# A fused attention, scan and expert kernel: four expert halves moved into the last scans, and the B and C rows stacked

## What is computed

```
x = x + attention(group_norm(x))                       # one head, 64 wide, softmax over 1024 points
t = tokens(x)
# layer 2, a state-space block on layer-normed tokens
z, xBC, dt = split(rms_norm(ln(t)) @ W_in.T)           # 256 | 256 + 32 + 32 | 8
xBC = silu(sum_k xpad[:, k:k+L] * conv_w[:, k] + b)    # causal, 4 taps, over 320 channels
xs, B, C = split(xBC)                                  # 8 heads of 32; B and C of 32 rows each
state = state * dA_t + (dt_t * x_t) outer B_t ; y_t = state . C_t
t = t + ln(t) + out_projection(rms_norm((y + D * xs) * silu(z)))
# layer 3, eight experts, two of them per token
u = ln(t); t = t + u + sum_e gate[e] * (gelu(u @ w1[e] + b1[e]) @ w2[e] + b2[e])
```

## Time and profile before

| | us |
|---|---|
| median of three runs | 1034.85 (1026.72, 1034.85, 1034.92) |
| profiled execution, its own time | 1039.91 |
| its span on the core | 1037.9 |
| PE busy | 889.0 (86%) |
| DVE busy | 742.6 (72%) |
| ACT busy | 522.2 (50%) |
| POOL busy | 250.3 (24%) |
| mean granted PE clock | 0.928 of 2.4 GHz |

### The profile page before, as it was taken

One profiled execution on the slowest core, in us unless ns is written; L12 is line 12 of the kernel. 1 busy time (PEld: TensorE's weight loads), 2 busy tenths in 40 slices (PEclk: granted clock), 3 DMA queues, 4 the chain that ended last, 5 costly groups with the idle time before them and its releaser, 6 DMA issues.

```text
span 1037.9 us, 19619 instructions
## 1 busy us (share of the span) xinstructions
PE 889.0 (86%) x7534; PEld 693.8 (67%) x7534; DVE 742.6 (72%) x1959; ACT 522.2 (50%) x795; POOL 250.3 (24%) x250
## 2 busy tenths in 40 slices
PE   3788998899887789788989797979788999889997
PEld 1555665655574567676768675757667888778887
DVE  2767677767765477686867777766768878787885
ACT  1534544544575464646464656454325654566543
POOL 0034111011100425242524252527511110011100
PEclk9889999999998679898988898989989999999999
DMA  4530000000000330303030303031000000000001
GB/s 138 178 130 22 20 2 21 21 11 12 21 1 15 57 70 3 71 2 71 2 71 1 72 2 71 2 71 63 2 1 1 22 21 22 1 21 22 21 2 42
DMA packets 30892, 36.13 MB, mean 35 GB/s; under 512 B 4560, under 2 KB 24912, under 8 KB 30800
## 3 DMA queue, kind: packets, MB, share of 16 engines
q1 hardware_dynamic: 29648, 30.68, 12.1%
q10 hardware_dynamic: 1152, 4.19, 1.1%
HBM read 21.50 MB, written 4.98 MB: 26 GB/s over the span
## 4 chain that ended last, share of the span: by engine, by line
PE 57%; DVE 27%; ACT 6%; issue 6%; POOL 2%; DMA 1%; SPq 1%; DVEq 0%; ACTq 0%; POOLq 0%
PE ps L1017 7%; PE ps L689 6%; DVE cacc L1665 4%; PE ps L939 4%; PE ps L768 3%; DVE acc L1942 3%; PE ps L770 3%; PE ps L769 3%; PE ps L676 3%; DVE nmax L1522 3%; PE ps L643 2%; PE ps L930 2%; ACT un L1335 2%; PE ps L890 2%; PE ps L648 2%
## 5 line engine op out<-in xcount | busy, mean ns | idle before, releaser
L1942 DVE SCALAR_TENSOR_TENSOR acc<-ps,comb,acc 128x128 f32<-128x128 f32 x512 | 141.1, 343 | 22.2 <-PE ps L1017 21.7
L1017 PEld LDWEIGHTS ps<-w_f,hid 128*128 128x128 f32 x1024 | 131.2, 191 | 16.4 <-ACT hid L1354 8.0
L1017 PE MATMUL ps<-w_f,hid 128*128 128x128 f32 x1024 | 136.7, 276 | 4.6 <-ACT hid L1354 4.5
L1354 ACT ACTIVATE hid<-ps,b_f 128x512 f32<-128x512 f32 x128 | 86.2, 685 | 107.6 <-PE ps L770 107.5
L1522 DVE TENSOR_REDUCE nmax<-ps 128x1 f32<-128x1024 f32 x64 | 78.1, 1221 | 39.7 <-PE ps L648 39.3
L559 POOL TENSOR_TENSOR srs<-sve,neg_half 128x1 f32<-128x1 f32 x64 | 50.9, 795 | 222.7 <-DVE gram L1774 222.7
L1665 DVE SCALAR_TENSOR_TENSOR cacc<-ps,cw,cacc 128x1023 f32<-128x1023 f32 (+5 forms) x72 | 91.8, 1275 | 8.5 <-ACT cacc L1238 7.5
L1295 ACT ACTIVATE dcy<-ps 128x1024 f32<-128x1024 f32 x64 | 65.1, 1017 | 62.3 <-PE ps L890 62.1
L1154 ACT ACTIVATE probs<-ps,nmax 128x1024 f32<-128x1024 f32 x64 | 71.3, 1114 | 41.1 <-DVE nmax L1522 38.2
L1757 DVE SCALAR_TENSOR_TENSOR dcy<-dcy,g_sb 128x1024 f32<-128x1024 f32 x64 | 86.2, 1346 | 1.0 <-ACT dcy L1295 1.0
L676 PEld LDWEIGHTS ps<-id_f,probs 128*128 128x128 f32 x512 | 59.7, 144 | 32.6 <-issue 22.9
(11 more groups left out here) (211 smaller groups left out, 1918.0 us busy)
## 6 DMA issues: line engine op xcount, KB each, us to landing
c_dec<-exp_dram SPq DMA_DIRECT2D x32, 256.0 KB, 5.3
xc<-in_x SPq DMA_DIRECT2D x8, 512.0 KB, 3.5
q_b<-q_a SPq DMA_DIRECT2D x16, 256.0 KB, 2.8
X<-in_x_tok ACTq DMA_DIRECT2D x8, 512.0 KB, 5.9
c_rep<-cacc SPq DMA_DIRECT2D x32, 128.0 KB, 4.9
out<-o_ch SPq DMA_DIRECT2D x8, 512.0 KB, 2.6
w_f<-in_w SPq DMA_DIRECT2D x2, 512.0 KB, 3.7
cst_f<-in_sel_rows SPq DMA_DIRECT2D x1, 512.0 KB, 5.2
```

The source lines that it names most:

```text
L1017: last = nc.tensor.matmul(ps[:, Y_BANKS[n], t * P:(t + 1) * P], hid[n % 2][:, t * P:(t + 1) * P], w2_f[:, e, :], start=True, stop=True)
L1354: nc.scalar.activation(hid[n % 2][:], ps[:, 4 + n % 2, :], ACT.Gelu, bias=b1_f[:, n // 2:n // 2 + 1]).then_inc(e_hidden_ready, 1)
L1942: done = nc.vector.scalar_tensor_tensor(acc[u][:, tt, :], ps[:, bank, t * P:(t + 1) * P], comb[u][:, tt, e:e + 1], acc[u][:, tt, :], ALU.m ...
```

## The change

B and C of a picture are laid so that partitions 0 to 63 hold B and C of the first 512 tokens and partitions 64 to 127 those of the last 512, in one bank. `w_half` holds the weights of group 2 with the other 64 columns zero; six matmuls of 512 columns add both halves into one bank, and three of 4 columns put the end of the first half in front of the second, for the taps. Tap, convolutions and silu then run over 128 x 512. B is turned from partitions 0 to 31 and, behind a wait, from 64 to 95; the copies of C are eight transfers. In the lists, `cumulate` on PE goes from slot 7 to 7.5, and on DVE `conv(2, 2)` goes from 7.5 to 7 and `exponents` from 7 to 7.5.

For the first picture's experts the statistics and the split of w1 and the router go to scan 6 (6.5 and 5.5), POOL's norm to its chunk 7; the rest of `scores` goes one slot earlier in the last scan, PE's parts two slots earlier; the first four halves are issued in the last scan and its tail, with their second products in banks 3, 2, 0 and 1, and DVE's first two weighted sums behind the last chunk.

```diff
+        w_half = [[sb(f"w_half{k}{part}", [P, P], F32R) for part in range(2)] for k in range(2)]
...
+        EARLY = 4
+        def second_bank(b, n):
+            if b == 0 and n < EARLY:
+                return (3, 2, 0, 1)[n]
+            return (3, 6, 7)[n % 3] if n < 2 * NE - 1 else 6
...  # SP, decay_rows
                 for h in range(4):
-                    sp.dma_start(c_rep[h * DS:(h + 1) * DS], cacc[b % 3][DS:2 * DS, 2, :]).then_inc(m_c_spread, 16)
+                    for part in range(2):
+                        r = slice((2 * part + 1) * DS, (2 * part + 2) * DS)
+                        sp.dma_start(c_rep[h * DS:(h + 1) * DS, part * BANK:(part + 1) * BANK],
+                                     cacc[b % 3][r, 2, 0:BANK]).then_inc(m_c_spread, 16)
...  # POOL, scan
+                    if b == B - 2 and c == NT - 1:
+                        norm(0, 0)
                     if last and c == 1:
-                        norm(0, 0)
-                    if last and c == 2:
                         start_sum(0, 0)
...  # PE, group
+                if g < 2:
+                    last = split(group_banks(b, g)[:, h, :], (w_xh[:, g, :], w_xl[:, g, :]), (xh[:, r], xl[:, r]))
+                elif h == 0:
+                    for part in range(2):
+                        q = slice(part * BANK, (part + 1) * BANK)
+                        hi, lo = w_half[0][part], w_half[1][part]
+                        nc.tensor.matmul(group_banks(b, 2)[:, 1, :], hi[:], xh[:, q], start=(part == 0), stop=False)
+                        nc.tensor.matmul(group_banks(b, 2)[:, 1, :], hi[:], xl[:, q], start=False, stop=False)
+                        nc.tensor.matmul(group_banks(b, 2)[:, 1, :], lo[:], xh[:, q], start=False, stop=(part == 1))
+                else:
+                    edge = slice(BANK - DCONV, BANK)
+                    last = split(group_banks(b, 2)[:, 0, edge], (w_half[0][1][:], w_half[1][1][:]), (xh[:, edge], xl[:, edge]))
...  # PE, turn_b
+                    if t == 3:
+                        last.then_inc(m_b_half_turned, 1)
+                        pe.wait_ge(m_b_half_turned, b + 1)
...  # PE, scan of the last picture
-                    elif c == 3:
+                    elif c == 1:
                         pe.wait_ge(m_x_gathered, 3 * B)
                         turn_tokens(0)
-                    elif c == 4:
+                    elif c == 2:
                         ...
                         logits(0, 0)
-                    elif c == 6:
+                    elif c == 4:
                         turn_weights(0, 0)
-                    elif c == 7:
+                    elif c == 5:
                         second_biases(0)
+                        pe.wait_ge(m_decay_ready, NT * B)
+                        expert(0, 0, 0)
+                        expert(0, 0, 1)
+                    elif c >= 6:
+                        second(0, c - 6, True)
+                        expert(0, 0, c - 4)
...  # pe_parts
-                        (group, (2, 0), 2, 5.5), (group, (2, 1), 2, 5.5), (cumulate, (), 2, 7)]
+                        (group, (2, 0), 2, 5.5), (group, (2, 1), 2, 5.5), (cumulate, (), 2, 7.5)]
...  # PE, second
+                if b == 0 and n < EARLY:
+                    if n >= 1:
+                        pe.wait_ge(e_bias_added, 1)
+                elif b == 0 and n == EARLY:
+                    pe.wait_ge(m_out_added, NT * B)
...  # ACT, scan of the last picture
+                    elif c == 0:
+                        token_norm(0)
                     elif c == 2:
-                        token_norm(0)
-                    elif c == 3:
                         token_high(0, 0)
+                    elif c == 4:
+                        gate_exponentials(0)
                     elif c == 5:
-                        gate_exponentials(0)
+                        gelu(0, 0)
+                        gelu(0, 1)
+                    elif c >= 6:
+                        gelu(0, c - 4)
...  # DVE, low_weights (in the attention of picture 6)
+                for halves, w in zip(w_half, (w_xh, w_xl)):
+                    for part in range(2):
+                        own, other = (slice(2 * DS * k, 2 * DS * (k + 1)) for k in (part, 1 - part))
+                        nc.vector.tensor_scalar(halves[part][:, other], id_f[:, other], 0.0, None, ALU.mult)
+                        nc.vector.tensor_copy(halves[part][:, own], w[:, 2, own].bitcast(F32))
...  # DVE, conv
+                    if g < 2:
+                        dst, src = cacc[b % 3][:, g, k:N], banks[:, 0:N - k]
+                    else:
+                        dst, src = cacc[b % 3][:, 2, 0:BANK], banks[:, BANK - k:N - k]
+                    ins = nc.vector.scalar_tensor_tensor(dst, src, cw[:, g, DCONV - 1 - k:DCONV - k], dst, ALU.mult, ALU.add)
...  # dve_parts
-                         ("exponents", (), 2, 7), ("conv", (2, 1), 2, 7), ("conv", (2, 2), 2, 7.5)]
+                         ("conv", (2, 1), 2, 7), ("conv", (2, 2), 2, 7), ("exponents", (), 2, 7.5)]
...  # DVE, scan
-                    parts = [(statistics, (), 1.5), (split_weights, (), 3.5), (low, (), 3.5), (largest, (), 4.5),
-                             (places, (), 4.5), (softmax, (), 5.5), (weights, (), 5.5), (turned, (), 6.5),
-                             (biases, (), 7.5)]
+                    parts = [(split_biases, (), 0.5), (low, (), 2.5), (largest, (), 3.5),
+                             (places, (), 3.5), (softmax, (), 4.5), (weights, (), 4.5), (turned, (), 5.5),
+                             (biases, (), 6.5), (weighted_sum, (0, 0, 0), 7.5), (weighted_sum, (0, 0, 1), 7.5)]
+                elif b == B - 2:
+                    parts = [(split_weights, (), 5.5), (first_scores[0], (), 6.5)]
```

More of the change, by code:

```diff
@@ L229, in hybrid_kernel @@
         comb_t = esb("comb_t", [P, P], F32R)
+        hid = [esb(f"hid{u}", [P, BANK]) for u in range(2)]
         acc.append(esb("acc1", [P, NT, P]))
@@ L1016, in second @@
                 for t in range(4):
-                    last = nc.tensor.matmul(ps[:, Y_BANKS[n], t * P:(t + 1) * P], hid[n % 2][:, t * P:(t + 1) * P],
+                    last = nc.tensor.matmul(ps[:, second_bank(b, n), t * P:(t + 1) * P], hid[n % 2][:, t * P:(t + 1) * P],
                                             w2_f[:, e, :], start=True, stop=True)
@@ L1069, in experts @@
             def experts(b, u, first, last):
-                for n in range(2 * NE):
+                for n in range(2 if first else 0, 2 * NE):
                     second(b, n, first)
@@ L1237, in tap @@
                 act.wait_ge(m_group_product, 3 * b + g + 1)
-                nc.scalar.activation(two(cacc[b % 3][:, g, :]), banks, ACT.Identity, bias=cb[:, g:g + 1],
+                if g < 2:
+                    dst, src = two(cacc[b % 3][:, g, :]), banks
+                else:
+                    dst, src = cacc[b % 3][:, 2, 0:BANK], banks[:, 1, :]
+                nc.scalar.activation(dst, src, ACT.Identity, bias=cb[:, g:g + 1],
                                      scale=cw[:, g, DCONV - 1:DCONV]).then_inc(m_tap_ready, 1)
@@ L1363, in experts @@
             def experts(b, u, first, last):
-                for n in range(2, 2 * NE):
+                for n in range(EARLY if first else 2, 2 * NE):
                     gelu(b, n)
@@ L1794, in scan @@
                 if last:
-                    statistics, low, largest, places, softmax, weights, turned, biases = scores(0, 0)
-                    parts = [(statistics, (), 1.5), (split_weights, (), 3.5), (low, (), 3.5), (largest, (), 4.5),
-                             (places, (), 4.5), (softmax, (), 5.5), (weights, (), 5.5), (turned, (), 6.5),
-                             (biases, (), 7.5)]
+                    statistics, low, largest, places, softmax, weights, turned, biases = first_scores
+                    parts = [(split_biases, (), 0.5), (low, (), 2.5), (largest, (), 3.5),
[3 more added lines that the diff above has]
+                    parts = [(split_weights, (), 5.5), (first_scores[0], (), 6.5)]
                 for c in range(NT):
@@ L1927, in scores, with weighted_sum @@
                 return statistics, low, largest, places, softmax, weights, turned, biases
+            def weighted_sum(b, u, k):
+                e, h = k // 2, k % 2
+                if k == 0:
+                    dve.wait_ge(e_bias_added, b + 1)
+                    dve.wait_ge(e_gates_ready, b + 1)
+                dve.wait_ge(e_second_product, 2 * NE * b + k + 1)
+                if k >= 2:
+                    dve.wait_ge(e_added, 2 * NE * b + k - 1)
+                for t in range(4):
+                    tt = 4 * h + t
+                    done = nc.vector.scalar_tensor_tensor(acc[u][:, tt, :], ps[:, second_bank(b, k), t * P:(t + 1) * P],
+                                                          comb[u][:, tt, e:e + 1], acc[u][:, tt, :],
+                                                          ALU.mult, ALU.add)
+                done.then_inc(e_added, 1)
```

(2 more changed lines are left out.)

71 lines of the change are left out of this document (31 added, 40 removed).

## The result

The changed kernel takes 1040.86 us in the median of 20 runs, the kernel before 1034.87 beside it: ratio 1.0072, 95% interval 1.0050 to 1.0093. That ratio leaves out the runs more than 1.5% above the fastest of their kernel; the two medians, of all runs, differ by 6.0 us, or 1.0058. The forecast was 1040. The profiled execution must be read with care: it took 1032.15 us (span 1030.1, mean granted clock 0.937), the fastest of its kernel, where the forecast for a profiled one was 1045, while the one before took 1039.91 at 0.928. By these two alone the change would look 8 us faster. So I compare stretches whose neighbours agree, and leave totals to the runs.

What follows compares the result with a forecast made beforehand. No engine bounds the program throughout; DVE and PE hand each other chunks, and who waits at which slot counts. Part 1 about 0 and part 2 +5 against the median 1034.85 gave 1040 us, range 1024 to 1051.

Steps and rivals of the forecast that it cites:

- Start of the scans: Before and in scan 0: shorter convolutions give -1.4 and -0.5, split-weight operations +0.5; together -1.4 us.
- part 1: The stacked B and C group, start of the scans plus five boundaries: about 0, between -8 and +5 us.
- Five boundaries: Scans 1 to 5: PE's wait before the cumulating matmuls returns before the gates, about 3.4 us; +0.3 each, +1.5 us.
- The drop of the clock: Behind PE's wait before the gates: a boundary gives -1.4 us at full clock, +0.6 if dropped; drop weighed three to one.
- a sign against it: At the boundaries: the forecast fails if the increments come over 1 us earlier.
- The wait among B's transposes: PE waits for its own first four transposes of B: 0.2 us taken, 0 to 0.5 possible.
- The copies of C: Rival, chance 0.15: inner products wait about 2 us for eight copies in each of six scans, +12; 1049 us.
- Scan 6: Weight split and statistics enter POOL-bound slots: scan 7 starts +2.4 us later, about +4 by the skill's interference rule.
- Scan 7: Last scan, PE's parts two slots forward, DVE's one: 47.7 us against 42.6, +5 at full clock, +9 at half; +6.5 taken.
- Experts: After the last output: second(4) at +1.8 us, about 3 us wait for next tokens, second(6) at 9.2 for 12.95; -3.75.
- part 2: Experts begun early: scan 6 +2.4, scan 7 +6.5, experts -3.75; together +5 us.
- The rival of full clock: Boundary waits too short for a clock drop, scan 7 at about 0: sum -10 to -12, 1024 us; chance 0.20.

Runs made afterwards that it cites:

- part 1 alone: Kernel before with the stacked B and C group and moved list entries, experts as before: 1034.51 us, ratio 1.0001 to the kernel before.
- the gates behind: Changed kernel with the gates' first half at slot 0.5, behind the increments, instead of slot 0: 1037.13 us, ratio 1.0014 to the kernel before.
- measured alone: Kernel before with the first picture's experts moved into the last scans, B and C not stacked: 1038.52 us, ratio 1.0036 to the kernel before.
- PE one slot later: Changed kernel with PE's logits, gate turning, bias products and first experts one slot later in the last scan: 1031.56 us, ratio 0.9969 to the kernel before.
- the early statistics: PE one slot later, plus the second picture's statistics, norm and normalization inside scan 7: 1027.57 us, ratio 0.9943 to the kernel before.
- the same move of the gates: Gates' first half at slot 0.5 instead of 0: on the kernel before 1040.01 us, ratio 1.0073; on the changed kernel 1037.13 us, ratio 1.0014.

## Why the prediction was right, step by step

- **Start of the scans, -1.4.** The wait before the gates of scan 0 fell from 3.41 to 1.69 us, and the inner products wait 1.45 us for the copies of C, where 0.45 stood:
```profile
370.70 0.51 PE L780 MATMUL ps<-xh,w_zh 128*128 128x512 f32 x1 [1.69 <-DVE cacc L1721]
...
388.06 1.68 PE L903 MATMUL ps<-c_rep,cacc 32*128 32x128 f32 x16 [1.45 <-DMA c_rep<-cacc]
```
By the waits 1.72 are gained and 1.00 given back: 0.7 for the 0.5 I left. But the size is not settled: from the first y of scan 0 to that of scan 1 it took 60.21 us before and 57.72 after (-2.5), and 61.14 in part 1 alone, where the inner products wait 1.76 us. The rest of the 1.4 was not measured by itself.
- **Five boundaries, +1.5.** The wait returned where it was put: 3.90 us four times and 2.80 once, for 3.4. The 1.7 before the output product was not in the prediction. The drop of the clock, weighed three to one, came four times in five (0.76 us for the first matmul). From y of chunk 6 to y of the next chunk 0 the five boundaries took 12.69 us in the mean before and 12.72 after: +0.03 for +0.3, and part 1 alone measured 0. At the boundary that the prediction worked through, the increments start 9.03 us after the end of the last long convolution, for the 9.1 worked out at full clock and 10.51 before. That is 1.5 us earlier, more than the 1 us that the prediction names as a sign against it. In the mean of the five it is 0.4 (10.64 for 11.03), for the gates ran slow at the other four. The wait among B's transposes was sized too small: the eight take 0.98 to 1.18 us for 0.68 in most scans before, at least 0.3 for the 0.2 allowed, while the inner products take 1.68 to 1.71 for 2.05, which no term had.
- **The copies of C.** The rival needed waits of about 2 us in each of six scans. The inner products wait in two scans only, 1.45 and 0.79 us (2.2 in all). The same place of SP's queue in scan 4 after:
```profile
581.64 4.97 SPq L474 DMA_DIRECT2D c_rep<-cacc  x8
```
They are issued 4.0 us after the increments' start (577.61), where it was 1.5 (588.46 less 586.98), and over 4.97 us instead of 2.44. So most of the rival's 3.9 us of slack was used, as worked out, and it did not run out in scans 1 to 5; with the gates behind it did in three of them. With one issue at some 0.6 us and the median landing times, I estimate 8.4 us from the first issue to the last landing (4.4 and 4.0) for 6.8 before (1.9 and 4.9); the inner products start 8.5 us after the first issue (590.14) without a wait. The Trainium skill (DMA: Bandwidth & Descriptors, Rules for kernel authors) has two transfers to disjoint partition halves serialize, because they share the same engines. That the set of eight landed no sooner agrees, though here the halves are of partitions only at the source; that shared engines are the reason is not shown, for each copy landed sooner and what grew is the issuing on SP's queue.
- **Scan 6, +2.4.** From y of chunk 5 of scan 6 to the first y of scan 7 it took 15.21 us for 12.09: +3.1, nearly all of it in the step that got the split (7.15 us for 4.13). DVE's split there, and POOL beside it:
```profile
705.04 1.73 DVE L1890 CAST w_h<-w_f 128x1024 fp32r<-128x1024 f32 x1
...
707.30 1.23 DVE L1893 TENSOR_TENSOR w_l<-w_f,w_h 128x1024 fp32r<-128x1024 f32 x1
708.44 1.88 DVE L1894 TENSOR_TENSOR rw_s<-rw_f,rw_s 128x8 fp32r<-128x8 f32 x1
```
```profile
707.72 2.58 POOL L562 TENSOR_TENSOR xw<-xs,wend 128x1024 f32<-128x1024 f32 x1
```
The same two operations in the kernel before, apart from each other:
```profile
720.60 1.91 POOL L550 TENSOR_TENSOR xw<-xs,wend 128x1024 f32<-128x1024 f32 x1
```
```profile
748.66 0.15 DVE L1840 TENSOR_TENSOR rw_s<-rw_f,rw_s 128x8 fp32r<-128x8 f32 x1
```
POOL's xw takes 2.58 us for 1.91 beside DVE's subtraction, and the subtraction of eight columns takes 1.88 us for 0.15 and ends when xw does. The Trainium skill (SBUF — State Buffer, Who interferes with whom) has the later of two such operations wait for the earlier: that agrees here in both directions. The price to POOL was 0.7 us, not the 1.5 worked out by that rule, for only 0.8 us of the subtraction were left when xw began.
- **Scan 7, +5 at full clock, taken as +6.5.** 47.5 us for 42.6: +4.9. PE's waits came as sized: 1.98 before the logits (2), 6.02 before the turning (6), with a slow stretch behind each. That the 47.7 summed over the slots for full clock was met is luck. From y to y the two steps that hold these waits took 8.51 and 9.18 us for 7.3 and 7.7, +2.7 with their slow matmuls. The six others took 29.8 for 32.7, -2.9, among them 3.38 for the 4.7 in which PE was to wait for the norm; it did not. So more was lost behind the waits than the 1.5 us added for half clock, and the slots at full clock were sized 2.9 us too long.
- **Experts, -3.75.** Second(4) starts 1.67 us after the last output (1.8), PE waits 3.13 for the next tokens (3), second(6) starts 9.06 us after the last output for 12.95: -3.9.
- **Sum.** By these rows part 2 is 3.1 + 4.9 - 3.9 = +4.1 for +5; measured alone it is +3.7, and part 1 0. Together they measured 0.72% (0.50 to 0.93), some 5 to 10 us, and 6.0 by the medians. The intervals of the parts reach that far; whether the 2 to 4 us between are chance or the two parts cost each other something is not settled. That the total came within 1 us of 1040 is in part luck, since its terms were off by as much and more.

The rival of full clock failed at both of its conditions: the clock dropped at four boundaries in five, and scan 7 did not stay as it was. But a good part of its gain was near at hand: with PE one slot later the early experts pay, by 3 us against the kernel before (the interval just reaches no change) and by 6 with the early statistics.

## What to carry to other kernels

When the work of two engines is moved forward in a hand-written order, move the consumer's parts by no more slots than the producer's: here two slots against one put 8 us of waits (1.98 and 6.02) on an engine that executes in order, and the last scan got 7.6 us longer than with one against one. A wait that is taken away at one instruction can come back at others whose operands come from the same chain, here the output product and the gates, so look for what stands there before counting the gain. And whether a piece of work should stand before or behind a wait has no fixed answer: the same move of the gates cost 0.7% in one version and gained 0.4 to 0.6% in the other, by which engine the step was waiting for.

## What the runs showed of the hardware

In the runs of the changed kernel the time goes with the mean granted clock. The one at 0.938 took 1036.05 us and the one at 0.921 took 1047.0; the lowest and highest times, 1032.15 and 1048.32, came at 0.937 and 0.919. Which slots run slow differs from boundary to boundary (gate matmuls of 0.47 us at one and 0.77 at the others) and from run to run: at the boundary from scan 3 to scan 4 a wait of 2.80 us came before the 0.47 us, and in the run with PE one slot later, whose lists are the same there, a wait of 2.81 before 0.76. So two single profiles of versions that differ by less than 1% can point the wrong way, as these did: -8 us by the profiles, +6 by the medians.
